# Moving the coefficient loads of a spectral stage from SyncE's queue to ScalarE's

## The reference, cut to what matters

```
coeff = complex(xi[..., 0], xi[..., 1]) * sqrt_eig        # 64 sets, 256 l, 257 m
x = einsum('nlm,mlk->nkm', coeff, pct)                     # for each m: (64 x 2) x 256 l times 256 l x 256 k
u = irfft(x, n=512)                                        # later stages, with attention and the network
```

## Time and profile before

| | us |
|---|---|
| median of 3 runs | 1433.62 (1431.69 to 1435.23) |
| profiled execution | 1443.99, of which the span is 1442.0 |
| first stage, by the start of ScalarE's last copy | 321.87 |

### The profile page before, as it was taken

One profiled execution on the slowest core, in us unless ns is written; L12 is line 12 of the kernel. 1 busy time (PEld: TensorE's weight loads), 2 busy tenths in 40 slices (PEclk: granted clock), 3 DMA queues, 4 the chain that ended last, 5 costly groups with the idle time before them and its releaser, 6 DMA issues. The chain is left out here.

```text
span 1442.0 us, 30500 instructions
## 1 busy us (share of the span) xinstructions
PE 1343.2 (93%) x8813; PEld 1165.2 (81%) x8813; DVE 929.3 (64%) x2026; ACT 900.1 (62%) x1956; POOL 560.0 (39%) x1394
## 2 busy tenths in 40 slices
PE   5999777899899999999999999999999989899994
PEld 4777666679899999999999999999999979455552
DVE  1222222226687887887878878888788777667662
ACT  1222222235677777777777777777777767757672
POOL 0000000000455555555555555555555546622212
PEclk8999999999999999999999999999999999999997
DMA  9999999985453333443333434333343332000000
GB/s 357 425 425 424 425 425 425 426 331 177 158 150 76 93 85 81 100 84 82 93 77 95 84 80 100 81 83 87 81 98 84 81 89 61 32 13 9 9 3 5
DMA packets 88315, 219.69 MB, mean 152 GB/s; under 512 B 20784, under 2 KB 33724, under 8 KB 75900
## 3 DMA queue, kind: packets, MB, share of 16 engines
q1 hardware_dynamic: 78728, 190.33, 42.1%
q10 hardware_dynamic: 4164, 27.27, 4.5%
q0 software_dynamic: 5376, 1.52, 0.6%
HBM read 147.77 MB, written 72.68 MB: 153 GB/s over the span
## 5 line engine op out<-in xcount | busy, mean ns | idle before, releaser
L674 PE MATMUL ps_k<-sphi,Glo 128*128 128x256 f32 x1024 | 292.7, 286 | 0.0
L673 PE MATMUL ps_k<-splo,Ghi 128*128 128x256 f32 x1024 | 291.4, 285 | 0.0
L672 PE MATMUL ps_k<-sphi,Ghi 128*128 128x256 f32 x1024 | 289.0, 282 | 0.0
L261 PE MATMUL s1b<-pg,cg 128*128 128x256 f32 x1024 | 245.1, 399 | 42.2 <-DVE cg L231 40.3
L261 PEld LDWEIGHTS s1b<-pg,cg 128*128 128x128 f32 x1024 | 201.3, 200 | 88.4 <-issue 28.7
L231 DVE TENSOR_TENSOR cg<-xg,se 128x1024 f32<-128x1024 f32 x63 | 77.2, 1225 | 223.8 <-DMA pg<-in_pct_dram 215.8
L1426 POOL TENSOR_SCALAR ve<-var 128x2 f32<-128x2 f32 x64 | 13.9, 217 | 479.9 <-ACT squares L1036 479.7
L672 PEld LDWEIGHTS ps_k<-sphi,Ghi 128*128 128x128 f32 x1024 | 195.2, 191 | 2.4
L673 PEld LDWEIGHTS ps_k<-splo,Ghi 128*128 128x128 f32 x1024 | 193.6, 189 | 2.7
L674 PEld LDWEIGHTS ps_k<-sphi,Glo 128*128 128x128 f32 x1024 | 194.3, 190 | 0.0
L316 ACT COPY stage<-s1b 128x512 f32<-128x512 f32 x104 | 60.7, 585 | 169.6 <-PE s1b L261 166.9
(11 more groups left out here) (175 smaller groups left out, 3191.6 us busy)
## 6 DMA issues: line engine op xcount, KB each, us to landing
pg<-in_pct_dram SPq DMA_DIRECT2D x63, 1024.0 KB, 26.0
out_dram<-o SPq DMA_DIRECT2D x64, 512.0 KB, 2.8
xg<-in_xs_dram SPq DMA_DIRECT2D x63, 512.0 KB, 24.9
xt<-spec SPq DMA_DIRECT2D x60, 512.0 KB
spec<-stage ACTq DMA_DIRECT2D x52, 512.0 KB, 8.2
rrow<-rs SPq DMA_DIRECT2D x64, 128.0 KB
spec<-hold SPq DMA_DIRECT2D x12, 480.0 KB, 5.3
recs<-rec SPq DMA_DIRECT2D x16, 160.0 KB
```

The lines of the kernel that those rows point to most:

```text
L261: last = nc.tensor.matmul(bank[at * PARTS + part][:, m % 2, :], cg[:, b % SETS, m * 2 + h, :], pg[:, b, m * 2 + h, :], start=(h == 0), sto ...
L672: nc.tensor.matmul(out_ap, whi, mhi, start=(j == 0), stop=False)
L673: nc.tensor.matmul(out_ap, whi, mlo, start=False, stop=False)
L674: last = nc.tensor.matmul(out_ap, wlo, mhi, start=False, stop=(j == n - 1))
```

## The change

SP keeps the `xg` loads of groups 0 to 7 and those of the two halves of group 63. The `xg` loads of groups 8 to 62 are issued by ScalarE, each after its copies of the group eight before, whose slot it fills; so they stand in queue q10 with the stores. The `pg` loads stay where they are. No byte is added or taken away. Lines behind L176 move down by one, and those behind the inserted load by three: the copies stand at L317, the new load at L324, the stores at L328.

```
             def load(g, b):
-                sp.dma_start(xg[:, b], xs_in[:, bass.ds(g * GM * 2, GM * 2), :]).then_inc(loaded[b], 16)
+                if isinstance(g, int) and g < RING1:
+                    sp.dma_start(xg[:, b], xs_in[:, bass.ds(g * GM * 2, GM * 2), :]).then_inc(loaded[b], 16)
                 sp.dma_start(pg[:, b], pct_in[:, bass.ds(g * GM * 2, GM * 2), :]).then_inc(loaded[b], 16)
...
                         act.wait_ge(top_kept, 1)
+                if not isinstance(g, int) or g + RING1 < GROUPS - 1:
+                    act.dma_start(xg[:, b], xs_in[:, bass.ds((g + RING1) * GM * 2, GM * 2), :]).then_inc(loaded[b], 16)
                 if b % 2 == 1 and not held:
                     act.wait_ge(copied, g * PARTS + PARTS)
```

## The result

| | before | changed |
|---|---|---|
| median of 14 runs, us | 1431.64 (1428.61 to 1437.45) | 1440.13 (1437.14 to 1446.05) |
| profiled execution, us (span) | 1443.99 (1442.0) | 1438.79 (1437.0) |
| start of ScalarE's last copy, us | 321.87 | 330.39 |

The ratio is 1.0057, with a 95% interval of 1.0044 to 1.0070: slower, by 8.5 us between the medians.

What follows compares the result with a forecast made beforehand. Transfers were taken to bound the first stage, not the second. The end's +8.1 us and the hole's -0.8 gave +7.3 on a median of 1433.62: 1440.9 us, range 1432.5 to 1446.

Steps and rivals of the forecast that it cites:

- Issue costs nothing: ScalarE's 55 added load issues, 0.48 us each, 26 us in all, are covered by its 166.9 us of waiting.
- Equal packets, 12.3 us a pair in build-up: Engines alternate packets between q10 and q1; q10 falls behind, weights run ahead, and a pair takes 12.3 us instead of 9.9.
- The end: First stage's end: group 50 copied at 293.6, then TensorE needs 35.1 us for ten groups, ending at 329.9: +8.1 us.
- its ends: Limits: three fewer groups of weights ahead leave no loss; TensorE slower after a pause adds 2.8 us.
- The hole: Transfer gap at 19 to 22 us, lacking 2.0 us of bytes; moved loads fill 0.8: -0.8 us.
- Sum: Whole kernel: +7.3 us, 1451.3 us for the profiled execution, 1440.9 us against the median.
- What the profile would show: Signs in the changed profile: waits, store and weight landing times, transfer rate, and the last copy at 328 to 332.
- The rival of the same time: First stage stays bound by transfers because q10 keeps up; time stays the same, 1433 us; chance 21%.

Runs made afterwards that it cites:

- the kernel with held weights: Changed kernel, but SP issues a group's weights only after ScalarE's copies of the group six before, instead of TensorE's products of eight before; ratio 1.0007, end 324.30.
- the second pair of profiles: The kernel before and the changed one, both unaltered, profiled once more; ScalarE's last copy starts at 322.75 and 333.23.

## Why the prediction was right, point by point

- **Issue costs nothing**: right. The moved loads' issue takes 0.34 us median (0.48 assumed), and the kernel with held weights has the same issues and a ratio of 1.0007.
- **Equal packets, 12.3 us a pair in build-up**: right. 355 packets against 352, though equal counts don't show that the turns are of one packet each; waits for stores end at 103.92, 116.69 and 129.00, so pairs of 12.8 and 12.3 us:

```profile
103.92 0.58 ACT L317 COPY stage<-s1b 128x512 f32<-128x512 f32 x1 [4.11 <-DMA spec<-stage]
...
116.69 0.58 ACT L317 COPY stage<-s1b 128x512 f32<-128x512 f32 x1 [6.53 <-DMA spec<-stage]
...
129.00 0.58 ACT L317 COPY stage<-s1b 128x512 f32<-128x512 f32 x1 [8.48 <-DMA spec<-stage]
```

- **The end**: right in its path and in its terms. Group 50 is copied at 293.19 (292.8 with the hole taken off); weights moved by then are 60.0 groups (60.7); the last ten groups take 34.7 us without a pause (35.1). What the sum left out is the clock: group 52 ran after a pause at the lower level, and this moved group 54 from 294.4 to 295.66. The prediction had named it, with 2.8 us, among its ends. 0.4 more for the copy, 1.3 for the clock and 0.4 less for the ten groups lead from 329.1 to 330.39. (329.9 less 321.87 is 8.0; the prediction wrote 8.1.)
- **The hole**: 183 GB/s against 140 are 0.3 us, not 0.8, and the kernel before shows 216 by itself in another profile. There was no gain.
- **Sum**: +7.3 forecast, +8.5 between the medians and at the stage's end; +10.5 at the end in the second pair of profiles. That it comes so close is in part luck, as two profiles of the changed kernel differ by 2.8 us at that point.
- **What the profile would show**: waits for stores 152.4 us (50 and more: right); store landing 14.8 us (15 and more: just short); weights 11.2 (well under 20: right); rate 422 to 426 up to 300 us (425: right). VectorE's wait for loads was to fall below 150; it is 120.0 + 69.7 = 189.7. I had thought of the weights' share alone: the coefficients now come late as well, because their issue stands behind ScalarE's wait for stores.
- **The rival of the same time** rested on q10 keeping up. With equal packets it did keep up, and the time rose all the same, so its premise wouldn't have been enough: a stream that runs ahead costs, whichever it is. The prediction named the wait for stores as the way to the loss, and in the changed kernel the end of the last such wait does set when group 54 starts. The other runs say more generally: the order of the bytes, of which this wait is one effect.
- **The Trainium skill's rule** ("DMA: Bandwidth & Descriptors", "Issuing engines are not separate DMA queues"), that another issuer saves only issue time, is right on the gain, which is none here; it leaves out the loss: 1.0057.

Open: what is left, 4 to 5 us at the end, with the stores on GpSimd; the lower rate (412 to 422 GB/s in windows between 22 and 220 us) of several of these kernels; some 3 us of group 54's delay that the count of bytes leaves, 1.3 of them the clock's, and over 4 in the second profile; some 4 us of the loss with weights in small packets. No kernel tried here is measurably faster than the one before.

## What to carry to other kernels

Where one stage keeps the DMA engines full, as here, a second queue for loads added no rate; it decided whose bytes went first. The single queue moved the loads in the order in which they were needed, and a short second one for the stores gave these their turn; splitting the loads over both made one side run ahead (that with the larger packets, when both had them to send), and the stage ended later. Before such a split, count packets and bytes of each queue over a period, and at the end of the stage count the groups that the computing engine has left when its last wait is over.

## What the runs showed of the hardware

- Two full queues got as many packets each, whatever the packets' size: 355 against 352 with 62.6% and 39.0% of the time, and 583 against 579 beside a third queue.
- With all loads in packets of 4096 bytes the engines, always busy, moved 418 to 420 GB/s from 22 to 290 us, against 421 to 425 in the two profiles of the changed kernel.
- Three loads with rows of 4 and 8 bytes go with a hole in the transfers, 140 GB/s over three us, or 216 in the second profile; when ScalarE issued them at its start, the hole was gone (412) and the first ten us were slower, 218 GB/s against 279.
- After a pause of 3.95 us TensorE ran a group at the lower clock level (granted 0.50): 6.5 us, against 3.45 at the full one.
- Issuing on a full queue holds the issuing engine: the median of SP's issues was 1.8 us before, and 0.33 us for the weights in the changed kernel:

```profile
L179 SPq DMA_DIRECT2D pg<-in_pct_dram x63: 327/333/3325, 2.6 to 299.3; - x63
```
